# The last sequence of a softmax attention regrouped, and a value product placed ahead of the Q projection, in a fused four-layer kernel

## What is computed

```python
# layer 3: 16 heads of 64
q, k, v = split(xn @ w_qkv); q, k = rope(q), rope(k)
attn = softmax(q @ k.T * 64**-0.5); out = (attn @ v) @ w_out
# layer 4
h = silu((x @ w1.T) * w1_s) * ((x @ w2.T) * w2_s)
h = gelu((h @ h1.T) * h1_s); h = gelu((h @ h2.T) * h2_s)
y = (h @ w3.T) * w3_s
```

## Time and profile before

| | us |
|---|---|
| median of 3 runs | 1292.22 (1291.72 to 1292.61) |
| the profiled execution | 1292.3 |
| its span, first to last instruction | 1290.4 |
| PE busy | 1151.3 (89%) |
| DVE busy | 980.8 (76%) |
| ACT busy | 780.4 (60%) |
| POOL busy | 563.2 (44%) |

### The profile page before, as it was taken

One profiled execution on the slowest core, in us unless ns is written; L12 is line 12 of the kernel. 1 busy time (PEld: TensorE's weight loads), 2 busy tenths in 40 slices (PEclk: granted clock), 3 DMA queues, 4 the chain that ended last, 5 costly groups with the idle time before them and its releaser, 6 DMA issues.

```text
span 1290.4 us, 32081 instructions
## 1 busy us (share of the span) xinstructions
PE 1151.3 (89%) x10554; PEld 949.4 (74%) x10554; DVE 980.8 (76%) x2499; ACT 780.4 (60%) x2324; POOL 563.2 (44%) x719
## 2 busy tenths in 40 slices
PE   3888885798989779999999999999999976999997
PEld 2555554788888757777777777777777755999997
DVE  6688885588888666777778777778787745888885
ACT  2455552222222169988888988889898874444442
POOL 2777764445444544444444544445444412011112
PEclk9899997799999989999999999999999987999999
DMA  9000000000000000000000000000000000000000
GB/s 284 5 2 0 0 1 2 1 2 1 1 0 0 1 1 2 1 2 2 2 2 0 0 0 0 0 0 0 0 0 1 2 1 1 6 12 12 8 12 18
DMA packets 14303, 12.32 MB, mean 10 GB/s; under 512 B 1778, under 2 KB 12564, under 8 KB 13972
## 3 DMA queue, kind: packets, MB, share of 16 engines
q1 hardware_dynamic: 14228, 11.34, 2.8%
HBM read 9.24 MB, written 2.10 MB: 9 GB/s over the span
## 4 chain that ended last, share of the span: by engine, by line
PE 45%; DVE 19%; issue 13%; POOL 4%; ACT 2%; DVEq 1%; POOLq 0%; ACTq 0%
PE bank L170 10%; PE bank L955 10%; PE bank L1049 9%; PE bank L1062 5%; PE bank L1020 5%; DVE work L1035 4%; PE bank L819 3%; POOL rstd L344 2%; DVE stat L277 2%; DVE work L1215 2%; DVE work L1207 2%; DVE yn L293 1%; PE bank L774 1%; POOL X L349 1%; DVE fh_hi L1176 1%
## 5 line engine op out<-in xcount | busy, mean ns | idle before, releaser
L972 ACT ACTIVATE work<-bank,work 128x256 f32<-128x256 f32 x512 | 236.0, 473 | 67.1 <-DVE work L964 66.5
L964 DVE TENSOR_REDUCE work<-bank 128x2 f32<-128x512 f32 x256 | 164.2, 684 | 119.6 <-PE bank L955 119.6
L986 POOL TENSOR_TENSOR work<-work 128x512 f32<-128x512 f32 x64 | 66.7, 1042 | 291.3 <-DVE work L980 291.3
L938 POOL TENSOR_TENSOR work<-work 128x512 f32<-128x512 f32 x128 | 164.2, 1283 | 30.8 <-DVE work L930 20.5
L992 ACT ACTIVATE work<-work 128x256 f32<-128x256 f32 x384 | 161.7, 510 | 0.0
L1020 PE MATMUL bank<-ident,work 128*128 128x128 f32 x1024 | 142.2, 281 | 4.9 <-POOL work L986 1.6
L1020 PEld LDWEIGHTS bank<-ident,work 128*128 128x128 f32 x1024 | 113.3, 143 | 36.9 <-issue 24.8
L819 PE MATMUL bank<-WrT,moe_work 128*128 128x128 f32 x1024 | 138.6, 279 | 0.7 <-POOL moe_work L796 0.7
L342 POOL TENSOR_SCALAR ve<-mv 128x2 f32<-128x2 f32 x128 | 28.8, 225 | 243.4 <-DVE mv L282 243.4
L955 PE MATMUL bank<-work 32*128 32x256 f32 x2048 | 131.0, 393 | 3.5 <-DVE work L930 1.7
L1049 PE MATMUL bank<-work 128*64 128x256 f32 x1024 | 127.2, 390 | 6.9 <-DVE work L1035 6.9
(11 more groups left out here) (176 smaller groups left out, 2916.3 us busy)
## 6 DMA issues: line engine op xcount, KB each, us to landing
X<-in_x SPq DMA_DIRECT2D x4, 512.0 KB, 5.9
wF<-in_L_ffn_h_w SPq DMA_DIRECT2D x2, 1024.0 KB, 9.7
out<-X SPq DMA_DIRECT2D x16, 128.0 KB, 1.8
w_qkv<-in_L_attn_w_qkv SPq DMA_DIRECT2D x1, 1536.0 KB, 9.3
WrT<-in_L_ffn_Wr SPq DMA_DIRECT2D x1, 1024.0 KB, 4.9
w_out<-in_L_attn_w_out SPq DMA_DIRECT2D x1, 512.0 KB, 10.5
wF<-in_L_ffn_w_w SPq DMA_DIRECT2D x2, 256.0 KB, 8.5
rope_sin<-in_rope_sin SPq DMA_DIRECT2D x1, 256.0 KB, 3.2
```

The lines of the kernel that those rows point to most:

```text
L938: nc.gpsimd.tensor_tensor((QT if kind == "q" else KT)[:, p, a, :], rc[:, ru % 2, :], rs_[:, ru % 2, :], ALU.add).then_inc(c_rope, 1)
L964: nc.vector.tensor_reduce(nmax[:, QUAD * a + j, :], SB_[j][:, :].rearrange("p (t k) -> p t k", t=T), AX.X, ALU.max, negate=True).then_inc( ...
L972: ins = nc.scalar.activation(pr[:, a % 2, j, t, :], SB_[j][:, t * LEN:(t + 1) * LEN], ACT.Exp, bias=nmax[:, h, t:t + 1], accum_out=psum_[: ...
```

## The change

Steady groups: the first product with V (k = 0) of the group before moves from behind the K unit to between the V and the Q unit. The second stays behind K.

The last sequence: on PE the scores of group a + 1 go ahead of the turns of heads 0 and 1 of group a, the outputs of sequence 14 and the norm turn of sequence 13 go to bank 6 and no longer to a bank of the scores, and they wait for DVE's copies of the group before. In group 3 the feed-forward's input products for sequence 0 stand where the scores of a next group would. POOL rounds the weights in place of ACT, ten pieces of 128x512 in the four groups (3, 3, 2, 2), so h2's pieces have moved ahead too (before, ACT rounded the last four behind the attention). DVE splits the input of the feed-forward in group 3. The output of sequence 15 goes to bank 7; ACT does the tanh of the feed-forward ahead of the last copy of the attention. The norm of sequence 14 on PE moves into the first step of the feed-forward, and DVE's last two norm pieces of sequence 15 behind the splits of that step. The count of the ternary check moves to the start of the attention. The buffers of the feed-forward are laid out anew so that each lies on memory whose last reader is done.

```diff
-        YB = SB_[2]
+        def out_bank(i):
+            return PB[1] if i_is(i, SEQS - 1) else SB_[2]
...
-        def ffn_weights_scalar(act, pieces):
+        def ffn_weights_pool(pool, pieces):
             for k in pieces:
-                nc.scalar.activation(ffn_weights[k][1], ffn_weights[k][0], ACT.Copy).then_inc(d_whi, 1)
+                nc.gpsimd.tensor_copy(ffn_weights[k][1], ffn_weights[k][0]).then_inc(d_whi, 1)
...
-        EARLY_SLOTS = {0: (0, 1), 1: (2, 3), 2: (4, 5)}
+        WEIGHT_SLOTS = ((0, 1, 2), (3, 4, 5), (6, 7), (8, 9))
... POOL, sa_step
+                    if i_is(i, SEQS - 1):
+                        if a == 0:
+                            pool.wait_ge(s_w[FFN], 16 * 7)
+                            pool.wait_ge(c_junit, SEQS * UNITS_S)
+                            pool.wait_ge(c_exp, QUAD * QUADS * (SEQS - 1))
+                        ffn_weights_pool(pool, WEIGHT_SLOTS[a][:1])
                     sa_norm_pool(pool, i, a, 0)
+                    if i_is(i, SEQS - 1):
+                        ffn_weights_pool(pool, WEIGHT_SLOTS[a][1:])
... DVE, sa_step and behind it
-                    elif a in EARLY_SLOTS:
-                        ffn_weights_vector(dve, EARLY_SLOTS[a])
+                    else:
+                        if a == QUADS - 1:
+                            ffn_input_vector(dve, 0)
+                        ffn_weights_vector(dve, WEIGHT_SLOTS[a])
...
-            for k in range(1, len(n3)):
-                run_piece(3, n3, k, SEQS - 2, 0)
...
-            ffn_input_vector(dve, 0)
-            ffn_ternary_vector(dve)
-            run_piece(3, n3, 0, SEQS - 1, 1)
+            run_piece(3, n3, 1, SEQS - 2, 0)
             ffn_in_vector(dve, 0)
-            run_piece(3, n3, 1, SEQS - 1, 1)
-            ffn_weights_vector(dve, range(EARLY, EARLY + HID_T // 2))
-            run_piece(3, n3, 2, SEQS - 1, 1)
-            ffn_weights_vector(dve, range(EARLY + HID_T // 2, EARLY + HID_T))
-            run_piece(3, n3, 3, SEQS - 1, 1)
+            for k in range(2, len(n3)):
+                run_piece(3, n3, k, SEQS - 2, 0)
+            for k in range(2):
+                run_piece(3, n3, k, SEQS - 1, 1)
... DVE, ffn_step, behind the splits of f1
+                if i_is(i, 0):
+                    for k in range(2, len(n3)):
+                        run_piece(3, n3, k, SEQS - 1, 1)
... ACT, behind the attention
-            sa_pv_scalar(act, SEQS - 1, 1, QUADS - 1)
-            for t in range(T):
-                sa_out_scalar(act, SEQS - 1, t, SB_[2 + t])
-            norm_scalar(act, 3, SEQS - 2, SB_[0][:, 0:LEN])
             act.wait_ge(s_fs, 2)
             ffn_in_scalar(act, 0)
-            ffn_weights_scalar(act, range(EARLY, EARLY + HID_T))
+            sa_pv_scalar(act, SEQS - 1, 1, QUADS - 1)
+            act.wait_ge(c_y, T * SEQS)
+            for t in range(T):
+                sa_out_scalar(act, SEQS - 1, t, VB[:, t * E:(t + 1) * E])
... PE, sa_step
-                    sa_scores_tensor(pe, i, p, a)
+                    if more or a == 0:
+                        sa_scores_tensor(pe, i, p, a)
                     if last:
-                        for j in range(2, 4):
-                            sa_turn_tensor(pe, last[0], last[2], j)
+                        sa_turn_tensor(pe, last[0], last[2], 2)
+                        if not more and a - 1 in SA_Y_SLOTS:
+                            pe.wait_ge(y_ready[SA], T * (i - 1) + SA_Y_SLOTS.index(a - 1) + 1)
+                        sa_turn_tensor(pe, last[0], last[2], 3)
                     if more:
                         pe.wait_ge(c_pta, reached(2 * n))
                         sa_unit_tensor(pe, i + 1, 1 - p, a, "v", UB_["v"])
+                    if last:
+                        sa_pv_tensor(pe, *last, 0)
                     if more:
                         pe.wait_ge(c_ptv, reached(2 * (n - 1) + 1))
                         sa_unit_tensor(pe, i + 1, 1 - p, a, "q", UB_["q"])
                         pe.wait_ge(c_ptv, reached(2 * (n - 1) + 2))
                         sa_unit_tensor(pe, i + 1, 1 - p, a, "k", UB_["k"])
                     if last:
-                        for k in range(2):
-                            sa_pv_tensor(pe, *last, k)
+                        sa_pv_tensor(pe, *last, 1)
...
+                    if not more:
+                        if a < QUADS - 1:
+                            sa_scores_tensor(pe, i, p, a + 1)
+                        else:
+                            pe.wait_ge(d_w, 2)
+                            pe.wait_ge(c_exp, QUAD * QUADS * SEQS)
+                            ffn_in_tensor(pe, 0)
                     for j in range(2):
                         sa_turn_tensor(pe, i, a, j)
```

103 lines of the change are left out of this document (58 added, 45 removed).

## The result

The changed kernel takes 1272.55 us (median of 4 runs, 1269.78 to 1273.35), the kernel before on the same chip 1291.97. The ratio is 0.9849, with a 95% interval of 0.9836 to 0.9862. Forecast were 1268 and a range of 1259 to 1280. The profiled execution took 1273.35 with a span of 1271.5, 18.9 us less than before. Lines of the change have new numbers: what was L170, L955, L972, L992, L1020, L1028, L1035, L1049 is now L191, L976, L993, L1013, L1041, L1049, L1056, L1070.

A forecast was written before the change was run, and what follows sets the result against it. PE (97.30 us of 100 busy) was taken to bound steady groups with an output, ACT's chain groups 0, and a chain sequence 15. 11.2 + 9.3 - 0.5 + 6.4 - 2.5 = 23.9 off 1292.3 gave 1268, range 1259 to 1280.

The forecast's parts named there:

- step 1: Steady groups: first product with V ahead of Q fills Q's 0.40 us wait; net 0.31 a group, 11.2 us in sum (5.6 to 14).
- Step 2: Sequence 15, exponentials of group 0 to group 3: 25.5 us against 34.77, gain 9.3, less 0.5 for late roundings.
- Rival C: Sequence 15 gains half, as POOL's roundings and DVE's subtractions stretch each other: 1273.4, or 1277 with lower clock; chance 0.14.
- Step 3: From group 3's last exponentials in sequence 15 to the first product with h1: 15.3 us against 21.7, gain 6.4.
- Step 4: First feed-forward step, first to second product with h1: 16.3 us against 13.76, 2.5 given back through work pushed behind the gate.
- The wait that PE was to have ahead of the first product with h2: First feed-forward step: PE waits about 3 us there, until the last norm piece is over, behind the splits.
- D: Every steady group gains the full 0.40 us, 23.6 in place of 11.2, if head 1's turn doesn't bind: 1256; chance 0.09.
- B: Steady part gives nothing: ACT holds the output groups too, or the wait only moves from Q to K: 1279.6; chance 0.12.
- F: Steady groups: the wait stays where it is, since DVE's copies move along with PE; same time as B; chance 0.02.
- E: Slower: the moved product with V waits for ACT's copy of bank 0, delaying Q and all behind: up to 1298; chance 0.03.

## Why the prediction was right, and where it was off

The direction, the order of size and the places were right: 1268 against 1272.55. The sum of 23.9 came out as 18.9, and step 1 alone makes up 4.7 of the 5.0 us that are missing. That the others add up to so little is partly luck: they missed by +1.1, -1.9 and -0.4 us, and 0.9 come from the first stretch, in which the change has no part.

**Step 1: the mechanism held, one term was mis-sized.** The wait of the Q unit went as said, nothing new waited, groups 0 kept 8.66 us with the turns stretched from 1.20 to 1.35, by the 0.15 that the group gains (1.5 was forecast, with the gain of 0.31). The term that failed is the price of the change of work on PE: "0.09 more. Net 0.31 a group". 0.09 is only the way into the product. The prediction took eight products as half of sixteen, 0.94 us, and they hold PE for 1.01 to 1.02, twice. The price is 0.24, the gain 0.16, below the bound of 0.2 to 0.4 that was given for it. Group 3 gave 0.15 and not 0.19. 28 x 0.16 + 13 x 0.15 = 6.4, measured 6.5, within the 5.6 to 14 of the sum. A row of before could have warned: the earlier trace rows shows that the first matmul behind a change isn't like its neighbours, and a block split in two has two such places. The kernel with the products between Q and K measured that price alone, 0.34 where nothing is covered, and the ones with both products together gave 9.92 and then 9.86 us, 0.40 and 0.46 less than before: that is what the rest was worth where no block is cut.

**Step 2: right, and slightly too careful.** 24.84 us against 25.5. The three engines within 0.3 us of one another is what the rows show: ACT waits 0.39 to 0.58 for turns, PE 0.34 for ACT, DVE little. The 1.3 us for a low clock in group 0 did not come: PE rested 1.57 us and its matmuls ran at full speed. Without that term the forecast was 24.2, 0.6 too low. Groups 2 and 3 took 8.38 instead of 8.0 and 8.2: PE's scores, turns with their 0.34 of wait, products and output follow one another from 1027.31 to 1035.74, 8.43 us.

Rival C's mechanism is in the rows: roundings of 0.61 stretched to 1.08, subtractions of 0.69 to 0.87 and 1.09. The Trainium skill says so in "SBUF — State Buffer", section "Who interferes with whom", for a VectorE instruction with two SBUF inputs beside a GpSimd instruction that reads SBUF; here the trace agrees, and the run with POOL idle shows the subtractions unstretched. Its price didn't come, because from group 1 on PE is the later engine (its row at 1030.69 waits 0.34 us, its scores of group 2 not at all) and the stretched 0.6 us on DVE lie beside it. 0.5 us were in the sum for it; the path took none that can be told.

**Step 3: 15.3 forecast, 17.2 measured.** The chain was the right one, and from the scale vectors on the forecast 6.4 us are there to 0.1. Two terms were off. The forecast is 13.6 us at full clock and 1.7 for the clock. At full clock the stretch takes 14.44, as three kernels show: DVE's input split ends 1.18 after T and PE's first product starts 0.26 behind it, at 1.44 and not 1.0 (0.4), and the turns of heads 2 and 3 wait 0.34 for ACT's copy of head 0 and then take 1.0, for which the sum had 1.1 together. The clock cost 2.75 in the profiled execution, with 1.0 above the 1.7, and 1.45 in another profile of the same kernel, so that term is a matter of the run.

**Step 4: 2.5 forecast, 2.9 measured,** by the mechanism named, three norm pieces that each wait 1.2 to 1.5 us for POOL. The wait that PE was to have ahead of the first product with h2 came as two, 2.22 ahead of the input products of sequence 1 and 1.67 ahead of the norm's turn. Two terms were off and met by luck. The count came to 15.6 and 0.7 for a low clock; the step took 16.63 us at a clock of 1.00 and 16.69 at 0.80, so the clock cost nothing, and the count was 1.0 short: the waits for POOL were 1.54, 1.22 and 1.21 where it had 1.1 each, and the input split took 1.1 and not 0.75. Changing the order on DVE took back all but 0.3 (14.06 against 13.76 before the change).

**The rivals.** D is refuted: groups 0 kept their pitch. B and F are refuted for the change itself; B's wait moving from Q to K is seen in the kernel with DVE's copy moved instead. E did not come: in the steady groups PE waited nowhere ahead of the products with V. Its path, by which a later Q holds bank 5 and the turn of head 0 up, is real all the same: with both products ahead of Q it cost sequence 0 0.76 us of waiting in a group. That the price of a split can turn this edit into a loss was none of the rivals, and it is what the kernel with the product between Q and K shows, at 1.0041.

**Open:** what costs the 0.3 us at each new pass of the loop and the 0.15 us in the other groups 0 that it runs, before and after alike, and why the first 450 us differ by up to four us from profile to profile.

## What to carry to other kernels

A wait filled with work that was there anyway isn't free where the work has to be cut in two: price each place at which the engine changes from one kind of matmul to another (here 0.09 us on the way in, 0.07 for a block of eight beyond half a block of sixteen, and 0.10 behind it), and put the whole block into the gap if it may stand there. When an engine is past 97% busy, look for what is queued ahead of the copy that frees its next bank; here that was the next wait. At the seam between two stages, read the order on the engine that serves both, and read what PE's clock did there in several profiles before crediting an edit with it.

## What the runs showed of the hardware

- Eight products of 64 columns of weights in fp32 between split-precision projections hold PE for 1.01 to 1.02 us, sixteen for 1.87 to 1.92: by these figures a block costs an estimated 0.10 to 0.15 us beyond its matmuls. The same output products take 1.79 us behind a projection and 1.89 behind the products with V.
- PE's clock after a rest: after 1.57 us it stayed at its higher level, 2.4 GHz (32 matmuls in 2.01). After 2.38 us, in the same place with the same work around it, it stayed there in three profiles, and in four it was at 1.2 GHz for 15 to 24 of the next 24 matmuls, which then lie 0.21 apart and not 0.12. In two of these four, and in the kernel with the rounding on ScalarE (a rest of 2.18 us), the first 5 to 11 matmuls still ran 0.12 apart and the later ones 0.21: the fall can come after the work has begun again. In the first feed-forward step of the changed kernel run again PE rested 2.22 and 2.52 us, and its granted clock was 1.00 throughout.
- A GpSimd rounding of 128x512 and a VectorE subtraction of the same size stretch one another, 0.61 to 1.08 and 0.69 to 0.87 or 1.09 us. With GpSimd idle the subtraction takes 0.69.
- Groups that a loop runs last up to 0.15 us longer than the same groups written out (8.66 and 8.51), and TensorE starts 0.23 to 0.30 us late, waiting for nothing that the profile names, at each new pass of the loop.
